# Eight small sums to GpSimd, one large sum to VectorE, and new orders on four engines of a two-layer graph kernel

## The reference

```python
def _L0(x, adj, W_fc, W_attn):
    h = jnp.einsum('bni,oi->bno', x, W_fc)
    f1 = jnp.einsum('bno,o->bn', h, W_attn[0, :32])
    f2 = jnp.einsum('bno,o->bn', h, W_attn[0, 32:])
    scores = leaky_relu(f1[:, :, None] + f2[:, None, :], 0.2)
    attn = softmax(where(adj == 0, -1e9, scores), axis=2)
    return elu(jnp.einsum('bnm,bmi->bni', attn, x))

def _L1(x, adj):
    xn = x / sqrt(maximum(sum(x * x, -1, keepdims=True), 1e-12))
    a = einsum('btd,bsd->bts', xn, xn) @ adj.astype(float32)
    return einsum('btr,brd->btd', a, x)

x = _layernorm(x + _L0(x, adj, W_fc, W_attn))
x = _layernorm(x + _L1(x, adj))
```

## Time and profile before

| what | value |
|---|---|
| median of 3 runs | 379.62 us (377.65 to 380.71) |
| profiled execution, device time | 380.89 us |
| its span, first to last instruction | 379.1 us |
| TensorE busy | 327.4 us (86%) |
| VectorE busy | 330.5 us (87%) |
| ScalarE busy | 275.1 us (73%) |
| GpSimd busy | 194.7 us (51%) |

### The profile page before, as it was taken

How to read it: one execution, slowest core, us unless ns; L and a number is a source line. 1 busy time by engine, 2 the same in 40 slices (tenths; PEclk the granted TensorE clock), 3 DMA queues, 4 the chain that set the end, 5 groups by cost and what they waited for, 6 DMA issues and landing times. The chain is left out here.

```text
span 379.1 us, 6926 instructions
## 1 busy us (share of the span) xinstructions
PE 327.4 (86%) x2244; PEld 302.6 (80%) x2244; DVE 330.5 (87%) x1012; ACT 275.1 (73%) x593; POOL 194.7 (51%) x167
## 2 busy tenths in 40 slices
PE   3095999899898989999898989989898989999790
PEld 1084999889797979889797979879797979998780
DVE  4589959999999999999999999999999999957412
ACT  0468696868878787868878787878878787884342
POOL 3405564654547375554548375554648475645401
PEclk9998799999999999999999999999999999999896
DMA  6861071534434544533443543633443541210102
GB/s 210 237 165 55 12 211 35 134 112 113 128 95 114 165 112 123 156 112 91 135 109 113 167 112 112 165 113 75 148 114 112 168 111 58 57 57 0 57 17 93
DMA packets 33971, 42.41 MB, mean 112 GB/s; under 512 B 1136, under 2 KB 25744, under 8 KB 33936
## 3 DMA queue, kind: packets, MB, share of 16 engines
q0 software_dynamic: 16896, 25.17, 24.6%
q1 hardware_dynamic: 17040, 16.81, 14.2%
HBM read 33.59 MB, written 8.39 MB: 111 GB/s over the span
## 5 line engine op out<-in xcount | busy, mean ns | idle before, releaser
L616 PE MATMUL ps_h<-x_hi,probT_hi 128*128 128x256 f32 x256 | 79.8, 312 | 0.4 <-issue 0.4
L617 PE MATMUL ps_h<-x_lo,probT_hi 128*128 128x256 f32 x256 | 72.8, 284 | 0.0
L618 PE MATMUL ps_h<-x_hi,probT_lo 128*128 128x256 f32 x256 | 72.6, 284 | 0.0
L600 PE MATMUL ps_probT<-ident,prob 128*128 128x128 f32 x256 | 41.6, 289 | 33.4 <-ACT prob L465 30.7
L646 PE MATMUL ps_l<-xn_hi,adj_sb 128*128 128x256 f32 x256 | 66.0, 297 | 2.1 <-POOL xn_lo L249 2.1
L600 PEld LDWEIGHTS ps_probT<-ident,prob 128*128 128x128 f32 x256 | 30.7, 148 | 43.8 <-ACT prob L465 35.2
L249 POOL TENSOR_TENSOR xn_lo<-xn,xn_hi 128x1024 fp32r<-128x1024 f32 x16 | 40.0, 2502 | 49.9 <-ACT xn_hi L499 49.9
L682 PE MATMUL ps_l<-w_sb,xnT 128*128 128x256 f32 x256 | 65.2, 380 | 0.3
L647 PE MATMUL ps_l<-xn_lo,adj_sb 128*128 128x256 f32 x256 | 63.3, 287 | 0.0
L669 PE MATMUL ps_l<-xn,z_sb 128*128 128x256 f32 x256 | 57.9, 379 | 0.0
L485 ACT ACTIVATE exp_h<-ps_h,rden 128x256 f32<-128x256 f32 x64 | 30.3, 474 | 36.9 <-PE ps_h L618 27.6
(11 more groups left out here) (52 smaller groups left out, 691.2 us busy)
## 6 DMA issues: line engine op xcount, KB each, us to landing
adj_sb<-adj POOLq DMA_DIRECT2D x16, 1024.0 KB, 5.9
x_sb<-x SPq DMA_DIRECT2D x16, 512.0 KB, 4.7
x_hi<-x POOLq DMA_DIRECT2D x16, 512.0 KB, 4.1
out<-o_sb SPq DMA_DIRECT2D x16, 512.0 KB, 3.1
attn_cols<-w_attn SPq DMA_DIRECT2D x2, 0.1 KB, 1.6
wfc<-w_fc SPq DMA_DIRECT2D x1, 32.0 KB, 1.7
```

Source lines behind the costliest of these rows:

```text
L600: last = nc.tensor.transpose(ps_probT[c % 2][:, k * P:(k + 1) * P], prob[:, c, k * P:(k + 1) * P], ident[:])
L616: nc.tensor.matmul(ps, probT_hi[:, c, blk], x_hi[n][:, k, :], start=(k == 0), stop=False)
L617: nc.tensor.matmul(ps, probT_hi[:, c, blk], x_lo[n][:, k, :], start=False, stop=False)
L618: last = nc.tensor.matmul(ps, probT_lo[:, c, blk], x_hi[n][:, k, :], start=False, stop=(k == NC - 1))
```

## The change

Four things are done together.

1. `residual_sum` leaves GpSimd. VectorE makes the same sum with a `tensor_tensor` of 128x1024 right behind `residual`, after a wait for that instruction.
2. The four small instructions of `row_moments` and `row_moments2` (L377, L379, L418, L419) leave VectorE. GpSimd makes them in `shifted_moments` and `shifted_moments2`.
3. GpSimd's order: `load_x_hi` is called first and for one graph more ahead, `split_xn` goes to the end of the step of the graph before, `shifted_moments2` stands ahead of `split_x`, and `shifted_moments` behind `shift2`.
4. The loops of VectorE, ScalarE and TensorE are written in a new order.

On GpSimd:

```diff
-            def residual_sum(g):
...
-                pool.wait_ge(q_ok, g + 1)
-                pool.tensor_tensor(y[n][:], y[n][:], exp_h[:], ALU.add).then_inc(y_ok, 1)
+            def shifted_moments(g):
...
+                pool.wait_ge(mv_ok, g + 1)
+                pool.tensor_scalar(moments[n][:, 0, :], mv[n][:, :, 1], LN_EPS, None,
+                                   ALU.add).then_inc(moments_ok, 1)
+                pool.tensor_scalar(moments[n][:, 1, :], mv[n][:, :, 1], float(D), LN_EPS * NORM_EPS, ALU.mult,
+                                   ALU.max).then_inc(moments_ok, 1)
...
+            def shifted_moments2(g):
...
+                pool.wait_ge(mv2_ok, g + 1)
+                pool.tensor_scalar(ve2[n][:], mv2[n][:, :, 1], LN_EPS, None, ALU.add).then_inc(ve2_ok, 1)
+                pool.tensor_scalar(neg_mean2[n][:], mv2[n][:, :, 0], -1.0, None, ALU.mult).then_inc(ve2_ok, 1)
...
             for i in STEPS:
-                split_xn(i)
-                load_x_hi(i + 2)
+                load_x_hi(i + 3)
                 norm(i)
                 load_adj(i + 3)
-                residual_sum(i + 1)
+                shifted_moments2(i - 1)
                 split_x(i + 2)
                 power2(i - 1)
                 shift2(i - 1)
+                shifted_moments(i + 1)
                 power(i + 1)
+                split_xn(i + 1)
```

On VectorE, behind the `scalar_tensor_tensor` of `residual` and in `row_moments` and `row_moments2`:

```diff
+                dve.wait_ge(q_ok, g + 1)
+                nc.vector.tensor_tensor(y[n][:], y[n][:], exp_h[:], ALU.add).then_inc(y_ok, 1)
...
-                dve.wait_ge(mv_ok, g + 1)
-                nc.vector.tensor_scalar(moments[n][:, 0, :], mv[n][:, :, 1], LN_EPS, None,
-                                        ALU.add).then_inc(moments_ok, 1)
-                nc.vector.tensor_scalar(moments[n][:, 1, :], mv[n][:, :, 1], float(D), LN_EPS * NORM_EPS, ALU.mult,
-                                        ALU.max).then_inc(moments_ok, 1)
...
-                dve.wait_ge(mv2_ok, g + 1)
-                nc.vector.tensor_scalar(ve2[n][:], mv2[n][:, :, 1], LN_EPS, None, ALU.add).then_inc(ve2_ok, 1)
-                nc.vector.tensor_scalar(neg_mean2[n][:], mv2[n][:, :, 0], -1.0, None, ALU.mult).then_inc(ve2_ok, 1)
```

More of the change, by code:

```diff
@@ L249, in split_xn @@
                 pool.tensor_tensor(xn_lo[n][:], xn[n][:], xn_hi[n][:].bitcast(F32), ALU.subtract).then_inc(xn_lo_ok, 1)
+            def shifted_moments2(g):
+                if not graph(g):
+                    return
+                n = g % NBUF
+                pool.wait_ge(mv2_ok, g + 1)
+                pool.tensor_scalar(ve2[n][:], mv2[n][:, :, 1], LN_EPS, None, ALU.add).then_inc(ve2_ok, 1)
+                pool.tensor_scalar(neg_mean2[n][:], mv2[n][:, :, 0], -1.0, None, ALU.mult).then_inc(ve2_ok, 1)
             def power2(g):
@@ L416, in row_moments2 @@
                 last.then_inc(mv2_ok, 1)
-                dve.wait_ge(mv2_ok, g + 1)
-                nc.vector.tensor_scalar(ve2[n][:], mv2[n][:, :, 1], LN_EPS, None, ALU.add).then_inc(ve2_ok, 1)
-                nc.vector.tensor_scalar(neg_mean2[n][:], mv2[n][:, :, 0], -1.0, None, ALU.mult).then_inc(ve2_ok, 1)
             for i in STEPS:
[L422 to L439, removed]
                 probT_lo_part(i + 1, 3)
-                masked_f2(i + 2, 0)
                 residual2(i - 1, 0)
                 masked_f2(i + 2, 1)
+                masked_f2(i + 2, 2)
+                residual2(i - 1, 1)
+                residual2(i - 1, 2)
+                negate_max(i + 2, 0)
+                masked_f2(i + 2, 3)
+                residual2(i - 1, 3)
+                node_scores(i + 3, 1)
+                negate_max(i + 2, 1)
+                residual(i + 1)
+                row_moments2(i - 1)
+                probT_lo_part(i + 2, 0)
+                row_moments(i + 1)
+                probT_lo_part(i + 2, 1)
+                node_scores(i + 3, 0)
+                denominators(i + 2)
+                make_mask(i + 3)
+                normalise(i + 1)
+                probT_lo_part(i + 2, 2)
+                masked_f2(i + 3, 0)
         @block.scalar
@@ L539, in _ @@
             for i in STEPS:
[L540 to L569, removed]
+                elu_exp(i + 1, 2)
+                elu_exp(i + 1, 3)
+                elu_relu(i + 1, 2)
+                elu_relu(i + 1, 3)
+                scale_z(i, 0)
+                scale_z(i, 1)
+                softmax_exp(i + 2, 0)
+                scale_z(i, 2)
+                softmax_exp(i + 2, 1)
+                scale_z(i, 3)
+                copy_xnT(i, 0)
+                probT_hi_part(i + 2, 0)
+                copy_xnT(i, 1)
+                copy_w(i, 0)
+                probT_hi_part(i + 2, 1)
+                softmax_exp(i + 2, 2)
+                lrelu(i + 2, 3)
+                softmax_exp(i + 2, 3)
+                copy_w(i, 1)
+                probT_hi_part(i + 2, 2)
+                elu_exp(i + 2, 0)
+                normalise2(i - 1)
+                elu_relu(i + 2, 0)
+                probT_hi_part(i + 2, 3)
+                xn_hi_part(i + 1)
+                elu_exp(i + 2, 1)
+                elu_relu(i + 2, 1)
+                lrelu(i + 3, 0)
+                lrelu(i + 3, 1)
+                lrelu(i + 3, 2)
         @block.tensor
@@ L686, in _ @@
             for i in STEPS:
[L687 to L694, removed]
                 make_w(i - 1, 0)
+                transpose_prob(i + 1, 1)
                 make_w(i - 1, 1)
-                transpose_prob(i + 1, 1)
+                bcast_f2(i + 2)
                 transpose_prob(i + 1, 2)
+                attend(i + 1, 0)
                 make_out(i - 1, 0)
-                attend(i + 1, 0)
+                transpose_prob(i + 1, 3)
                 make_out(i - 1, 1)
-                transpose_prob(i + 1, 3)
-                bcast_f2(i + 2)
                 attend(i + 1, 1)
                 make_out(i - 1, 2)
+                attend(i + 1, 2)
+                attend(i + 1, 3)
+                make_out(i - 1, 3)
+                make_z(i, 0)
+                make_z(i, 1)
+                make_z(i, 2)
+                make_z(i, 3)
+                transpose_prob(i + 2, 0)
+                transpose_xn(i, 0)
+                transpose_xn(i, 1)
 def kernel(x, adj, L0_gnn_W_fc, L0_gnn_W_attn):
```

## The result

The changed kernel takes 365.67 us (median of 4 runs, 364.94 to 366.5) against 379.59 us of the kernel before in the same comparison. The ratio is 0.964, with a 95% interval of 0.959 to 0.968. The profiled execution took 365.61 us with a span of 363.8 us.

What follows compares the result with a forecast made beforehand. VectorE, with its blocked instruction, was taken to set the 21.44 us step. Eleven steps at 20.1 gain 14.7 us, less 2.5 in filling, plus 0.5 at the end: 12.7 us, so 366.9 us; range 357 to 376.

Steps and rivals of the forecast that it cites:

- The loop: From VectorE's row_moments2 through GpSimd's sums and power back to VectorE's normalise; claimed a 20.1 us step.
- VectorE's own work: VectorE's step without waits, small sums removed and the large one added: 18.2 us, against 21.44 us a step before.
- the new sum: The residual sum as a tensor_tensor on VectorE: 1.25 us added a step, between 1.1 and 1.4.
- R: The end of row_moments2 on VectorE, from which the forecast counted the starts of mask, power and normalise.
- the rest: VectorE's step from normalise round to the end of row_moments2: 12.6 us.
- Either way `normalise` starts near R + 7.5: Whether mask or power starts first, the other waits, so VectorE's normalise starts 7.3 to 7.8 us after R.
- The first rival: Power starts ahead of the mask without stopping it, TensorE becomes the bound: step 19.5 us, time 360; chance 0.26.
- The ends of the pipeline: Filling and draining: 2.5 us lost in filling, 0.5 us gained at the end.
- 2.5 us for `load_x_hi(0)`: In filling, this load goes ahead of load_adj(0) in GpSimd's queue; first mask delayed by nothing to 4.9 us.
- The collision with `negate_max`: Second rival: L418's stall moves to negate_max or node_scores on VectorE; 0.7 us more a step, time 374.6; chance 0.19.
- free of collisions: VectorE's residual sum, with residual, was said to fall where GpSimd waits for make_z.
- A cost of up to 2.4 us: What the residual sum on VectorE would lose if it did collide with GpSimd's work.

Runs made afterwards that it cites:

- e4: The changed kernel with make_mask called behind normalise instead of ahead of it; 369.57 us, ratio 0.974.
- e6: The changed kernel with shifted_moments and power called ahead of power2 and shift2 on GpSimd; 370.27 us, ratio 0.978.
- e11: The changed kernel with only the first norm's two small sums back on VectorE; 355.65 us, ratio 0.937.
- e2: The kernel before with only the large residual sum moved to VectorE, small sums and orders as before; 376.76 us, ratio 0.995.
- e3: The kernel before with only the four small sums moved to GpSimd; 388.85 us, ratio 1.026.
- e8: The kernel before with the large sum on VectorE and negate_max of the second half ahead of residual; 354.26 us, ratio 0.936.
- e13: e8 with the second norm's two small sums put behind row_moments on VectorE; 388.11 us, ratio 1.022.
- e1: The changed kernel with all four small sums back on VectorE, large sum and new orders kept; 359.24 us, ratio 0.948.
- e12: The changed kernel with only the second norm's two small sums back on VectorE; 356.08 us, ratio 0.938.
- e9: e1 with the second norm's two small sums put behind row_moments on VectorE; 357.33 us, ratio 0.943.

## Why the prediction was right, and where its steps were off

The forecast was 366.9 us; 365.67 us was measured. The loop behind it was right. That the time came so close was luck in part: the steps gained less than forecast, the ends gained more, and the two errors nearly cancelled.

**The loop was read rightly, each term within some 0.2 us.** VectorE's own work is 20.33 - 2.19 = 18.1 us (forecast 18.2), the new sum 1.23 us (1.25), the mask at R + 4.3 (4.5), `normalise` at R + 7.7 (7.5), the rest 12.6 (12.6), the step 20.33 (20.1). The forecast signs of it, a wait of 1.5 to 2 us at `normalise` and a GpSimd instruction stretched by up to 1.1 us at the mask, stand in the profile at 2.19 us, a little above, and 0.85 us. e4 shows that the mask is the cause and what it costs GpSimd.

**"Either way `normalise` starts near R + 7.5" was wrong.** It assumed that a power that starts first would delay the mask. In e6 the mask isn't delayed and `normalise` starts at R + 5.6. The forecast held because the other order occurred, by the 0.2 us with which the mask started first. The first rival, TensorE as the bound, is what e11 shows, with the power ahead of the mask: 19.41 us a step (the rival's 19.5) and 355.7 us (360 forecast). But e11 has two small sums back on VectorE. In the changed kernel with all of them moved, putting the power first wasn't enough: e6 has it and steps at 20.3, since `normalise2` then waits.

**The ends of the pipeline were mis-sized, and in the wrong direction.** I took 2.5 us for `load_x_hi(0)` ahead of `load_adj(0)`. The first mask came only 0.29 us later, and the start as a whole became 0.84 us shorter. The end gave 2.2 us where I had 0.5. Of these, 1.12 us are one more step (graph 13 to 14 took 20.07 us and takes 18.95), which the sum over eleven steps left out. The step from 14 to 15 gave 0.03 (18.37 to 18.34), although in the kernel before a `negate_max` had stood in it for 2.37 us (at 325.27). The other 1.05 us lie behind the last `residual`, and they come from the granted clock of TensorE and not from the calls: `xn_hi_part` of the last graph starts 10.01 us behind that `residual` in the kernel before and 10.06 us in the changed one, but the four z that follow take 5.39 us before (355.93 to 361.32) and 3.90 us after (341.75 to 345.65), 1.49 us less; the rest of the stretch is 0.4 us longer. The third value from the end of a row of windows is the granted clock. In the kernel before it stood at 0.50, the lower of the two levels (1.2 GHz), for 3.4 us of them:

```profile
356.25:359.65 3.40, 3.40 (x18) 3.40 (x17) 0.24 (x2) 0.66 (x2) 1.21 (x2) 0.50 0.02 5
```

In the changed kernel it stood at the upper one (2.4 GHz) all through:

```profile
341.70:345.70 4.00, 3.95 (x33) 3.98 (x34) 0.33 (x4) 1.43 (x3) 1.96 (x6) 1.00 0.02 4
```

TensorE had waited about as long just before, 2.07 us and 2.09 us, in both. In the filling, from 31 to 47 us, the granted clock was 0.79 before and 0.89 after, so part of the 0.84 us may be the same; that wasn't separated. The runs of the kernel before differ in this way too, in one comparison from 377.3 us at a mean granted clock of 0.983 to 381.1 us at 0.974. By the span I forecast 12.7 us, and 15.3 came: 2.4 too much in the steps, 5.0 too little at the ends. The term that was most wrong is the 2.5 us for `load_x_hi(0)`: the first mask shows 0.29.

**The collision with `negate_max` was a real rival.** I gave it 0.19 and said that it stands clear in the new order. It does, and e2 and e3 show what happens where it doesn't: it stands 2.3 and 2.9 us longer in each step, and freeing it, from e2 to e8, took 1.85 us off the step. What I had not seen is how thin the margins are, and what uses them up: a new sum ahead of `negate_max` (e2), or a wait for the power, which puts VectorE later against `load_adj` (e3, e13). I called the new sum free of collisions. In the changed kernel it starts 0.44 us ahead of the issue of `load_adj` (190.40 against 190.84); in e13 it starts 0.32 us behind it. "A cost of up to 2.4 us" for the large sum if it met GpSimd's was right in kind and too small: e13 shows 2.7 us of standing.

**The parts were not weighed against each other.** I listed the small sums as a gain of 4.1 us of VectorE work a step and the new sum as a cost. In truth the gain comes from taking the large sum off GpSimd with `negate_max` ahead of `residual` (e8); moving half of the small sums gives about 1% on top of the large sum and the orders (e1 against e11 and e12), and moving all of them gives back more than that through GpSimd's later power.

## What to carry to other kernels

When a tiny VectorE instruction lasts microseconds, look which GpSimd instruction ends with it; before removing it, or adding work near it, list the VectorE instructions with two SBUF inputs around it, ahead of it too, and their distance from GpSimd's large ones, since the next stall is at whichever of them then meets GpSimd. Here it paid to take the large operation off GpSimd rather than the small ones off VectorE. Check what GpSimd's later start does to whoever waits for its result. Test each part alone and the parts by halves: here two edits worth 0.5% and nothing gave 6.4% together, and the full change was beaten by four kernels that hold only a part of it (e1, e8, e11, e12). Take the granted clock of the ends before explaining a microsecond there.

## What the runs showed of the hardware that was not expected

**The mask and the power.** The power on GpSimd reads 8 numbers a partition and lasts 1.64 to 1.74 us with no mask in it (e1, the changed kernel and the kernel before). Started ahead of the mask it lets the mask run (1.19 and 1.20 us in e6, e9, e11 and e12), but it doesn't end before the mask does: in e12 it is stretched to 2.46 us and ends 0.04 us behind the mask, in e11 to 1.93 us (190.90 to 192.83, the mask to 192.79). In the changed kernel a small GpSimd sum that starts inside the mask ends 0.08 us behind it. The runs show these ends, not the reason. The Trainium skill, page "SBUF — State Buffer", section "Who interferes with whom", says that the first to start keeps the pair for the whole instruction. The large sums that VectorE's small instructions stand behind agree with it, the power, which starts first and doesn't stop the mask, doesn't.

**An issue of a transfer in front of a large sum.** In e3 and e13 a VectorE instruction with two SBUF inputs starts 0.12 and 0.32 us after GpSimd began to issue `load_adj`, 0.7 and 0.5 us before the large sum shown behind it starts (in e2 the two are 0.70 and 0.11 us), and yet it ends only after that sum: 0.03 us behind it in e3 (0.02 in e2), 1.1 us behind it in e13 (it lasts 1.23 us when it runs free). In e1 a `negate_max` starts just as early, 0.12 us into the issue of `load_x_hi`, behind which only small instructions stand, and lasts 0.21 us. So it isn't the issue alone that blocks. Whether the sum holds VectorE up while the issue still runs, or its start is shown too late, stays open.
